# A planned four-stage kernel: the last rows' end by tile, the last FFN block let past the one ahead, and new due times

## The chip, the cores and the metric

The kernel runs on one core of one Trainium2 chip. The metric is the device time of one execution in microseconds (us), the median of several. In the profile PE is TensorE (matmuls), PEld its weight loads, DVE is VectorE, ACT is ScalarE, POOL is GpSimd and SPq is SyncE's queue, from which all transfers are issued.

## The reference, cut to what is computed

The input x is 4 sequences of 1024 rows by 256 features, float32. Four sub-layers follow, each with a residual and a layer norm behind it: a linear attention (stage a), a gated FFN with dequantised weights (stage b), a differential softmax attention with 8 heads (stage c), and a small transformer of two layers (stage d), whose local attention and FFN are what the change touches. Of that last one:

```python
for l in range(2):
    qkv = shift_token(x) @ wqkv                    # 256 -> 3 * 512
    q, k = rotary_xpos(l2norm(q) * qs, l2norm(k) * ksc)
    o = local_attention(q, k, v)                   # 8 heads, windows of 128 rows, each sees itself and the one before
    x = x + o @ wo                                 # 512 -> 256
    h = layernorm(shift_token(x)) * lg + lb
    a, g = split(h @ w1 + b1)                      # 256 -> 2 * 682
    x = x + (a * gelu(g)) @ w2 + b2                # 682 -> 256
x = layernorm(x_before_the_two_layers + x)         # the end of the kernel
```

## The kernel before, in words

The activations x stay in SBUF, as 32 tiles of 128 rows by 256. Float32 products are made of three fp32r products of high and low parts, so an operand is first split: one copy that rounds (the high part) and one subtraction (the low part).

Stage d has, for each of its two layers, 32 windows (one for each tile) and 8 FFN blocks of 4 tiles (512 rows). Blocks are counted through both layers as b = 8 * l + bk, so block 15 is the last one and holds tiles 28 to 31, and block 14 is ahead of it. A window runs d_qk, d_v (projections), d_rope, d_turn, d_sim, d_max, d_exp, d_flip, d_w (attention), d_wo (output), a transfer d_hs that shifts the rows by one, and n_st / n_nm (statistics and normalisation for the FFN). A block runs f_x (two sets of 4 transposes, split into high and low), and then for j = 0 to 5 of the hidden columns f_g, f_a (6 matmuls each; for j = 5 one group holds both), f_ge (GELU on ACT), f_mul (DVE), a split of the hidden part, and f_down (12 matmuls that accumulate in two PSUM banks). f_add adds the two banks to x on DVE, four tiles together. In layer 1 f_r3 (POOL) adds the rows that were kept from ahead of stage d, and n_st / n_nm / store end the block: 4 tiles at a time, with one 512 KB transfer to the output.

The hidden part is split by POOL (f_hp: CAST and subtraction, L2355 and L2357), but in block 15 by ACT (f_hp, L1772) and DVE (f_hl, L2160). The same holds for the rows in f_x.

No engine chooses its order at run time. A planner (class Order) simulates stage d with a cost for each operation (TOOK) and writes each engine's order down. An operation has a due time, PERIOD * window + DUE[...] for windows and PERIOD * (4 * b + 3) + LATE + pace * k for the k-th product of a block. Of the operations that could start within EPS us of the first, the planner takes the one with the lowest due time; so a due time only decides between operations that are ready together. A weight piece is fetched by `fetch` into one of two buffers (SP w_in), is thought to land LANDS us after it, and is then copied on ACT and subtracted on POOL (w_out, L1593 and L2227). In layer 0 the w1 and w2 pieces have the due times FIRST + j * STEP. The engines' queues are in order: an ACT copy that waits for a late transfer holds back all that the planner put behind it.

The products of a block form a chain on PE, and the first of a block comes after the last f_down of the block ahead:

```python
put(len(chain), "pe", kind, *i, after=list(after) + chain[-1:] + ([("pe", "f_down", *before, 5)] if not chain and b else []),
```

SyncE's queue holds all eight stores behind everything else.

## Time and profile before

| | us |
|---|---|
| time, median of 3 runs | 2915.0 |
| lowest and highest | 2911.52, 2915.43 |
| the profiled execution's own time | 2915.99 |
| its span | 2914.1 |

The span is what the trace covers; the profiled execution's own time is 1.9 us longer, and 1.0 us over the median. Stage d begins near 1555 us of the span and takes the rest. PE is busy 97% of the span at a mean granted clock of 0.987, and the second-busiest engine, DVE, 74%.

### The profile page before, as it was taken

What the parts mean: (1) busy time and instruction counts of PE and PEld (TensorE: products, weight loads), DVE (VectorE), ACT (ScalarE), POOL (GpSimd) and SP (SyncE); (2) the same over time, 40 slices, a digit from 0 to 9 for tenths busy, and PEclk for the clock granted to TensorE, in tenths of its full rate; (3) what the DMA queues carried; (4) which work ended last, traced back from release to release, by engine and by line L of the source; (5) the groups of instructions that cost most, each with busy time, mean ns of one, the idle gap of its engine ahead of it and who ended that gap; (6) DMA issues with size and microseconds to landing.
All of it is one profiled execution on the core that took longest, in us unless ns stands there. A gap on an engine that the chain in (4) does not pass through costs nothing.

```text
span 2914.1 us, 52525 instructions
## 1 busy us (share of the span) xinstructions
PE 2819.9 (97%) x20384; PEld 1898.0 (65%) x20384; DVE 2169.0 (74%) x5057; ACT 1651.0 (57%) x3486; POOL 1049.7 (36%) x1208
## 2 busy tenths in 40 slices
PE   8998999999999999999998899999999999999997
PEld 7777877433333333333335778888888878888886
DVE  7885545788788778877874667777777778888884
ACT  3222332665565656556664666666666766666662
POOL 5343442014113211321322334444545554444451
PEclk9999999999999999999999999999999999999998
DMA  2000010320321222042202000000000100000001
GB/s 79 23 9 23 8 22 3 40 28 10 41 23 17 29 28 28 6 59 23 35 11 80 23 5 5 4 5 5 11 27 19 33 27 4 12 11 12 12 11 60
DMA packets 49100, 66.64 MB, mean 23 GB/s; under 512 B 12542, under 2 KB 37076, under 8 KB 48852
## 3 DMA queue, kind: packets, MB, share of 16 engines
q1 hardware_dynamic: 48852, 63.29, 12.2%
q8 instruction: 161, 2.64, 0.4%
q14 instruction: 87, 0.71, 0.1%
HBM read 24.99 MB, written 8.39 MB: 11 GB/s over the span
## 4 chain that ended last, share of the span: by engine, by line
PE 86%; DVE 6%; ACT 3%; DMA 2%; POOL 1%; issue 1%; SPq 1%; POOLq 0%; DVEq 0%; ACTq 0%
PE ps L1394 17%; PE pw L219 17%; PE ps L219 12%; PE pw L1381 11%; PE ps L1180 5%; PE pw L1180 5%; PE ps L1554 4%; PE pw L1467 3%; PE pw L1505 2%; PE pw L1487 1%; PE pw L1330 1%; PE ps L1467 1%; PE ps L1505 1%; PE ps L1487 1%; DMA c_qst<-c_mr 1%
## 5 line engine op out<-in xcount | busy, mean ns | idle before, releaser
L1682 ACT ACTIVATE c_p<-pw 128x512 f32<-128x512 f32 x1024 | 562.3, 595 | 340.5 <-PE ps L1364 183.9
L1394 PE MATMUL ps<-c_p,c_vals 128*64 128x512 f32 x2048 | 548.1, 619 | 3.5 <-ACT c_p L1682 2.2
L1968 DVE TENSOR_REDUCE c_mx<-ps 128x1 f32<-128x512 f32 x694 | 462.7, 683 | 114.1 <-PE ps L1364 106.8
L1381 PEld LDWEIGHTS pw<-c_qst,c_kst 50*128 50x128 f32 x1024 | 154.6, 185 | 368.4 <-ACT c_p L1682 271.9
L1381 PE MATMUL pw<-c_qst,c_kst 50*128 50x512 f32 x1024 | 385.1, 450 | 9.6 <-DMA c_qst<-c_mr 8.4
L1364 PE MATMUL ps<-c_kst,c_qst 48*128 48x512 f32 x694 | 289.3, 452 | 4.4 <-DMA c_kst<-shared 3.5
L1736 ACT ACTIVATE e_sm<-e_sm,e_mx 128x256 f32<-128x256 f32 x512 | 253.9, 498 | 61.8 <-DVE e_mx L2113 61.7
L1968 DVE TENSOR_REDUCE c_mx<-pw 128x1 f32<-128x512 f32 x330 | 225.5, 683 | 47.8 <-PE pw L1364 43.4
L2336 POOL TENSOR_TENSOR e_ss<-e_ss,half 128x16 f32<-128x16 f32 x64 | 186.4, 2912 | 127.9 <-DVE e_ss L2070 84.7
L1394 PEld LDWEIGHTS ps<-c_p,c_vals 128*64 128x64 f32 x2048 | 104.5, 135 | 182.1 <-issue 162.2
L2233 POOL TENSOR_SCALAR stat<-stat 128x1 f32<-128x1 f32 (+1 forms) x138 | 32.2, 233 | 518.1 <-DVE stat L1840 471.5
L219 PE MATMUL pw<-shared,e_xb 128*128 128x512 f32 x774 | 213.1, 412 | 2.3 <-DVE e_xb L2062 1.6
L219 PE MATMUL pw<-shared,e_w 128*124 128x512 f32 (+1 forms) x774 | 204.5, 405 | 1.5 <-ACT e_ge L1781 1.3
L2296 POOL TENSOR_TENSOR c_o<-c_o,c_t 128x128 f32<-128x128 f32 x32 | 14.6, 455 | 487.9 <-DVE c_t L2014 487.9
L2113 DVE CUSTOM_DVE_ANT_0 e_sm<-pw,e_mask,e_ss 128x256 f32<-128x256 f32 x336 | 145.1, 477 | 27.3 <-PE pw L1467 15.3
L1554 PE MATMUL ps<-e_w,e_hp 124*128 124x256 f32 (+1 forms) x1152 | 158.9, 286 | 6.2 <-POOL e_hp L2357 4.6
L219 PEld LDWEIGHTS pw<-shared,e_w 128*124 128x124 f32 (+1 forms) x774 | 140.1, 188 | 36.0 <-ACT e_of L1753 1.5
L219 PEld LDWEIGHTS pw<-shared,e_xb 128*128 128x128 f32 x774 | 138.6, 191 | 30.4 <-DVE e_xb L2062 1.8
L1554 PEld LDWEIGHTS ps<-e_w,e_hp 124*128 124x128 f32 (+1 forms) x1152 | 142.3, 189 | 11.5 <-POOL e_hp L2357 5.3
L1364 PE MATMUL pw<-c_kst,c_qst 48*128 48x512 f32 x330 | 148.7, 450 | 0.0
L1467 PE MATMUL pw<-e_k,e_qt 64*128 64x128 f32 x1344 | 127.9, 280 | 2.6 <-ACT e_pt L1744 1.8
L1364 PEld LDWEIGHTS ps<-c_kst,c_qst 48*128 48x128 f32 x694 | 117.0, 185 | 17.4 <-issue 7.9
(316 smaller groups left out, 6343.5 us busy)
## 6 DMA issues: line engine op xcount, KB each, us to landing
c_kst<-shared SPq DMA_DIRECT2D x192, 64.0 KB
c_qst<-shared SPq DMA_DIRECT2D x64, 128.0 KB
x<-in_L_attn_x SPq DMA_DIRECT2D x8, 512.0 KB, 3.8
c_qst<-shared SPq DMA_DIRECT2D x64, 64.0 KB
keep<-x SPq DMA_DIRECT2D x8, 512.0 KB, 4.0
e_raw<-keep SPq DMA_DIRECT2D x8, 512.0 KB, 3.5
out<-x SPq DMA_DIRECT2D x8, 512.0 KB, 4.7
e_hs<-x SPq DMA_DIRECT2D x64, 63.0 KB
```

Of the source, the lines that this page charges most:

```text
L219: ins = e.matmul(o, l, r, start=first and n == 1, stop=n == 3 * len(parts), skip_group_check=True)
L1180: ins = e.transpose(o, v, ident[0:v.shape[0], 0:v.shape[0]])
L1364: e.matmul(bank_of("c_max", n, sh, qt, h), c_qst[i][p0:p0 + 48, sh // 2, 128 * qt:128 * qt + 128], c_kst[i][p0:p0 + 48, sh // 2, 512 * h:5 ...
L1381: e.matmul(bank_of("c_s", n, sh, kt, h), c_kst[i][p0:p0 + 50, sh // 2, 128 * kt:128 * kt + 128], c_qst[i][p0:p0 + 50, sh // 2, 512 * h:512 ...
L1394: ins = e.matmul(pv[64 * h:64 * h + 64, :], c_v[:, kt, 33 * hd:33 * hd + 64], p[:, 512 * h:512 * h + 512], start=kt == 0, stop=kt == 7, sk ...
L1467: ins = e.matmul(p[r][:, c0:c0 + 128], qt[rs, hb, :], kk[rs, hb, :], start=True, stop=True, skip_group_check=True)
L1554: ins = e.matmul(o, hp[kk, l_, 128 * i:128 * i + 128], d_w2[kk, r, j, :], start=j == 0 and i % 2 == 0 and n == 0, stop=j == 5 and n == 2, ...
L1682: e.activation(c_p[slot["c_p", (n, sh, kt)]][:, 512 * h:512 * h + 512], bank_of("c_s", n, sh, kt, h), ACT.Exp, scale=0.5).then_inc(SC, 1)
L1736: e.activation(sm[:, q, :], sm[:, q, :], ACT.Exp, bias=mx[:, 0, q:q + 1], scale=-1.0, accum_out=mx[:, 1, q:q + 1]).then_inc(SC, 1)
L1968: e.tensor_reduce(c_mx[m % 2][:, qt, h:h + 1], bank_of("c_max", n, sh, qt, h), AX.X, ALU.max).then_inc(VE, 1)
L2113: e.tensor_tensor_reduce(d_sm[s][:, q, :], p[:, 256 * h:256 * h + 256], d_mask[:, 1 if win % 8 else 0, :], st[:, 2, head:head + 1], 3.0e38 ...
L2336: e.tensor_tensor(st[:, 1, :], st[:, 0, :], half[:, :], ALU.pow).then_inc(GP, 1)
```

## The change

It has four parts. (1) The last FFN block by tile: the last f_down of block 15 signals once after its first PSUM bank and again after its second; then f_add, n_st, n_nm and store go tile by tile (stage name "g", tiles 28 to 31), with four transfers of 128 KB in place of one of 512 KB. (2) Block 15's first product no longer has to come after block 14's last f_down, so the planner may put block 15's first products ahead of block 14's last ones; and the hidden parts j = 4 and 5 of block 14 are split by ACT and DVE in place of POOL (`hurried`). (3) LANDS goes from 3.2 to 2.91, FIRST from 10 to 14.83, STEP from 18 to 21.95. (4) LATE and some 25 entries of DUE get new values, so all engines' orders in stage d are planned anew.

```diff
--- before.py
+++ after.py
@@ -16,7 +16,7 @@
 TURN = (0, 2, 1, 3)
-PERIOD, LATE, SPREAD, EPS, LAG = 21, 63.6, 1.36, 0.13, 0.05
+PERIOD, LATE, SPREAD, EPS, LAG, LANDS, FIRST, STEP = 21, 63.09, 1.36, 0.13, 0.05, 2.91, 14.83, 21.95
 TOOK = {"pe d_x": 0.44, "act d_x": 0.62, "dve d_x": 0.72, "dve d_xs": 0.1, "pe d_qk": 1.5, "act d_qk": 0.62,
@@ -33,21 +33,22 @@
-        "dve n_st c": 0.6, "pool n_st c": 0.8, "dve n_nm c": 0.4, "dve n_st b": 3.8, "pool n_st b": 1.4, "dve n_nm b": 1.7,
+        "dve n_st g": 0.6, "pool n_st g": 0.85, "dve n_nm g": 0.42, "dve n_st c": 0.6, "pool n_st c": 0.8, "dve n_nm c": 0.4, "dve n_st b": 3.8, "pool n_st b": 1.4, "dve n_nm b": 1.7,
 BY_HALF = ("d_sim", "d_max", "d_exp", "d_flip", "d_soft", "d_w")
-DUE = {"pe d_qk": 13.7, "act d_qk": 3.7, "dve d_rope": 12.8, "pe d_turn": 5.6, "act d_turn": -19.7, "dve d_ss": 43.6,
+DUE = {"pe d_qk": 13.8, "act d_qk": -0.3, "dve d_rope": 13.2, "pe d_turn": 3.5, "act d_turn": -15.3, "dve d_ss": 31,
-       "pe d_sim1": 19.9, "dve d_max0": 14.6, "dve d_max1": 21.3, "act d_exp0": 16.5, "act d_exp1": 30.3,
-       "pe d_flip0": 5.5, "pe d_flip1": 32.2, "act d_flip0": 31.6, "act d_flip1": -0.2, "dve d_soft0": 20.7,
-       "dve d_soft1": -6.3, "pe d_w0": 25, "pe d_w1": 11.2, "pe d_rb": 42.8, "act d_rb": -19, "dve d_o": 26,
-       "act d_o": 30.9, "dve d_ol": 37.9, "pe d_wo": 15.7, "dve d_wo": 38.1, "dve n_st": 49.9, "pool n_st": 33.8,
-       "dve n_nm": 43.9, "d_x": -1.4}
-LANDS, FIRST, STEP = 3.2, 10, 18
+       "pe d_sim1": 19.9, "dve d_max0": 13.3, "dve d_max1": 28.9, "act d_exp0": 21, "act d_exp1": 30.1,
+       "pe d_flip0": 3.3, "pe d_flip1": 32.2, "act d_flip0": 33.8, "act d_flip1": -6, "dve d_soft0": 20.2,
+       "dve d_soft1": -12.6, "pe d_w0": 23.9, "pe d_w1": 16, "pe d_rb": 43.6, "act d_rb": -34.4, "dve d_o": 28,
+       "act d_o": 43, "dve d_ol": 37.9, "pe d_wo": 21, "dve d_wo": 36.2, "dve n_st": 50, "pool n_st": 38.1,
+       "dve n_nm": 48.7, "d_x": -0.2}
@@ -354,6 +355,10 @@
 
+        def hurried(l, bk, j):
+            return l == 1 and (bk == 7 or bk == 6 and j >= 4)
@@ -972,7 +977,7 @@
 
-                    put(len(chain), "pe", kind, *i, after=list(after) + chain[-1:] + ([("pe", "f_down", *before, 5)] if not chain and b else []),
+                    put(len(chain), "pe", kind, *i, after=list(after) + chain[-1:] + ([("pe", "f_down", *before, 5)] if not chain and 0 < b < 15 else []),
                         **rings)
@@ -987,11 +992,10 @@
                 rows_split = ("dve", "f_xl", *n, 1) if b == 15 else ("pool", "f_x", *n, 1)
-                part_split = ("dve", "f_hl") if b == 15 else ("pool", "f_hp")
 
                 def down(j):
-                    product("f_down", j, after=[(*part_split, *n, j), ("pool", "w_out", ("w2", l, j, 0))],
-                            takes=[(acc, "f_acc", *n, k) for k in range(2 if j == 0 else 0)], gives=[(hps, "f_hp", *n, j)])
+                    product("f_down", j, after=[("dve", "f_hl", *n, j) if hurried(l, bk, j) else ("pool", "f_hp", *n, j), ("pool", "w_out", ("w2", l, j, 0))],
+                            n_of=2 if b == 15 and j == 5 else 1, takes=[(acc, "f_acc", *n, k) for k in range(2 if j == 0 else 0)], gives=[(hps, "f_hp", *n, j)])
 
@@ -1010,7 +1014,7 @@
                         takes=[(hfs, "f_hf", *n, j), (hps, "f_hp", *n, j)], gives=[(bank, both, *n, j)], place=ones if j == 5 else None)
-                    if b == 15:
+                    if hurried(l, bk, j):
                         put(len(chain), "act", "f_hp", j, after=[("dve", "f_mul", *n, j)])
@@ -1021,8 +1025,9 @@
                 hs_read = [("dma", "d_hs", l, t) for t in range(4 * bk, kept + 1)]
-                put(len(chain), "dve", "f_add", n_of=4, after=[("pe", "f_down", *n, 5)] + hs_read + [("pool", "f_r3", bk)] * l,
-                    gives=[(acc, "f_acc", *n, k) for k in range(2)])
+                added = [("pe", "f_down", *n, 5)] + hs_read + [("pool", "f_r3", bk)] * l
+                if b < 15:
+                    put(len(chain), "dve", "f_add", n_of=4, after=added, gives=[(acc, "f_acc", *n, k) for k in range(2)])
                 if l:
@@ -1033,9 +1038,17 @@
                     op(t, "pool", "f_r3", (bk,), 1, [("sp", "r3_in", bk), ("dve", "n_nm", "d", 1, 4 * bk + 3)] + hs_read)
-                    op(t, "dve", "n_st", ("f", bk), 8, [("dve", "f_add", 1, bk)])
-                    op(t, "pool", "n_st", ("f", bk), 2, [("dve", "n_st", "f", bk)])
-                    op(t, "dve", "n_nm", ("f", bk), 4, [("pool", "n_st", "f", bk)])
+                    if b < 15:
+                        op(t, "dve", "n_st", ("f", bk), 8, [("dve", "f_add", 1, bk)])
+                        op(t, "pool", "n_st", ("f", bk), 2, [("dve", "n_st", "f", bk)])
+                        op(t, "dve", "n_nm", ("f", bk), 4, [("pool", "n_st", "f", bk)])
+                        return
+                    for j in range(4):
+                        tile = ("g", 28 + j)
+                        op(t + j, "dve", "f_add", (*n, j), 1, added + [("dve", "f_add", *n, j - 1)] * (j > 0), took=0.44)
+                        op(t + j, "dve", "n_st", tile, 2, [("dve", "f_add", *n, j)])
+                        op(t + j, "pool", "n_st", tile, 2, [("dve", "n_st", *tile)])
+                        op(t + j, "dve", "n_nm", tile, 1, [("pool", "n_st", *tile)])
 
@@ -1101,7 +1114,7 @@
         for i in range(8):
-            P.land(f"x{i}", 1, "store", i)
+            P.land(f"x{i}", 4 if i == 7 else 1, "store", i)
             P.add("store", i)
@@ -1160,7 +1173,7 @@
         def norm_tiles(stage, i):
-            return [i[0]] if stage in ("a", "c") else [24 + 4 * i[0] + t for t in range(4)] if stage == "c4" else [
+            return [i[0]] if stage in ("a", "c", "g") else [24 + 4 * i[0] + t for t in range(4)] if stage == "c4" else [
                 4 * i[0] + t for t in range(4)]
@@ -1543,7 +1556,7 @@
                 w.wait_ge(*pool("w_out", ("w2", l, j, 0)))
-                w.wait_ge(*(dve("f_hl", l, bk, j) if (l, bk) == (1, 7) else pool("f_hp", l, bk, j)))
+                w.wait_ge(*(dve("f_hl", l, bk, j) if hurried(l, bk, j) else pool("f_hp", l, bk, j)))
                 if j == 0:
@@ -1553,7 +1566,8 @@
                                        start=j == 0 and i % 2 == 0 and n == 0, stop=j == 5 and n == 2, skip_group_check=True)
-                ins.then_inc(PE, 1)
+                    if i == 3 or (l, bk, j, i) == (1, 7, 5, 1):
+                        ins.then_inc(PE, 1)
 
@@ -1827,6 +1841,8 @@
                     w.wait_ge(*dve("f_add", 1, i[0]))
+                elif stage == "g":
+                    w.wait_ge(*dve("f_add", 1, 7, i[0] - 28))
                 elif stage != "d":
@@ -2178,12 +2194,12 @@
 
-            def f_add(l, bk):
-                w.wait_ge(*pe("f_down", l, bk, 5))
+            def f_add(l, bk, *one):
                 if l:
                     w.wait_ge(*pool("f_r3", bk))
-                for j in range(4):
+                for j in one or range(4):
                     tile = 4 * bk + j
+                    w.wait_ge(*of("pe", "f_down", (l, bk, 5), j // 2 + 1 if one else None))
                     w.wait_ge(*dma("d_hs", l, tile if tile % 8 == 7 else tile + 1))
@@ -2227,7 +2243,7 @@
             def n_st(stage, *i):
-                st, n = st_of(stage, *i), 1 if stage in ("a", "c", "d") else 4
+                st, n = st_of(stage, *i), 1 if stage in ("a", "c", "d", "g") else 4
                 w.wait_ge(*dve("ident"))
@@ -2490,8 +2506,13 @@
             def store(i):
-                w.wait_ge(*dve("n_nm", "f", i))
-                e.dma_start(xout[:, 4 * i:4 * i + 4, :], x[:, 4 * i:4 * i + 4, :]).then_inc(sems[f"x{i}"], 16)
+                if i < 7:
+                    w.wait_ge(*dve("n_nm", "f", i))
+                    e.dma_start(xout[:, 4 * i:4 * i + 4, :], x[:, 4 * i:4 * i + 4, :]).then_inc(sems[f"x{i}"], 16)
+                    return
+                for t in range(28, 32):
+                    w.wait_ge(*dve("n_nm", "g", t))
+                    e.dma_start(xout[:, t:t + 1, :], x[:, t:t + 1, :]).then_inc(sems["x7"], 16)
 
```

## Rows read from the trace of the kernel before

**Rows 1.** The page, part 1: busy us by engine, share of the span, instructions.
```profile
PE 2819.9 (97%) x20384; PEld 1898.0 (65%) x20384; DVE 2169.0 (74%) x5057; ACT 1651.0 (57%) x3486; POOL 1049.7 (36%) x1208
```

**Rows 2.** Windows: length, busy us of PE, PEld, DVE, ACT, POOL, clock, DMA.
```profile
1560.00:1720.00 160.00, 136.40 (x1139) 115.34 (x1138) 111.31 (x321) 93.19 (x234) 61.32 (x65) 0.92 0.13 40
1720.00:2240.00 520.00, 518.50 (x4484) 450.83 (x4482) 396.89 (x1059) 350.62 (x807) 235.64 (x252) 1.00 0.04 11
2240.00:2420.00 180.00, 174.47 (x1516) 150.70 (x1516) 136.06 (x346) 121.17 (x275) 90.08 (x93) 1.00 0.09 25
```

**Rows 3.** f_add in layer 0 and 1: count, ns min/median/max, first and last start.
```profile
L2188 DVE TENSOR_TENSOR x<-x,ps x16: 415/416/421, 1928.9 to 2169.3; 128x256 f32<-128x256 f32 x16
...
L2188 DVE TENSOR_TENSOR x<-x,ps x20: 412/414/422, 2415.9 to 2737.3; 128x256 f32<-128x256 f32 x20
```

**Rows 4.** Timeline, layer 0's start: start us, us, instruction, idle before and releaser.
```profile
1610.21 0.42 ACT L1593 ACTIVATE e_w<-e_raw 124x256 fp32r<-124x256 f32 x1 [1.12 <-DMA e_raw<-in_L_ffn_w]
...
1611.67 1.11 PE L1180 MATMUL ps<-ident,e_sm 128*128 128x128 f32 x4 [4.15 <-ACT e_sm L1736]
...
1630.90 2.10 PE L1180 MATMUL pw<-ident,e_sm 128*128 128x128 f32 x8 [4.04 <-ACT e_sm L1736]
```

**Rows 5.** Timeline, the last window's normalisation to block 15's first product.
```profile
2860.73 1.56 PE L219 MATMUL ps<-shared,e_w 128*126 128x512 f32 x6
...
2860.91 0.21 DVE L1840 BATCH_NORM_AGGREGATE stat<-stat 128x2 f32<-128x12 f32 x1
...
2862.11 0.61 DVE L1850 TENSOR_SCALAR e_hn<-x,stat 128x128 f32<-128x128 f32 x1 [0.34 <-POOL stat L2235]
...
2862.65 1.42 DVE L1850 TENSOR_SCALAR e_hn<-e_hs,stat 128x128 f32<-128x128 f32 x1
...
2862.73 1.26 POOL L2357 TENSOR_TENSOR e_hp<-e_hf,e_hp 124x512 fp32r<-124x512 f32 x1
...
2864.04 1.63 PE L1554 MATMUL ps<-e_w,e_hp 124*128 124x256 f32 x12 [1.74 <-POOL e_hp L2357]
...
2868.55 1.65 PE L1554 MATMUL ps<-e_w,e_hp 63*128 63x256 f32 x6 [2.88 <-POOL e_hp L2357]
...
2871.41 1.97 PE L1180 MATMUL pw<-ident,e_hn 128*128 128x128 f32 x8
...
2875.82 2.92 PE L219 MATMUL ps<-shared,e_w 128*124 128x512 f32 x6 [2.44 <-DVE shared L2155]
```

**Rows 6.** The same normalisation: 18 earlier ones, and one at 2339.
```profile
L1850 DVE TENSOR_SCALAR e_hn<-e_hs,stat x18: 333/342/660, 2515.9 to 2848.1; 128x128 f32<-128x128 f32 x18
...
2339.69 1.44 DVE L1850 TENSOR_SCALAR e_hn<-e_hs,stat 128x128 f32<-128x128 f32 x1
```

**Rows 7.** Windows of the end: behind POOL stand granted clock, DMA share, GB/s.
```profile
2862.00:2864.00 2.00, 0.30 (x2) 0.00 (x0) 1.89 (x2) 0.68 (x1) 1.91 (x3) 1.00 1.04 335
2870.00:2880.00 10.00, 7.56 (x25) 6.00 (x25) 5.92 (x16) 1.95 (x3) 1.28 (x2) 0.50 0.01 2
2882.00:2900.00 18.00, 18.00 (x104) 15.54 (x103) 8.31 (x16) 6.04 (x10) 0.00 (x0) 1.00 0.09 29
```

**Rows 8.** Timeline of the final product, additions, statistics and normalisation.
```profile
2902.84 1.67 PE L1554 MATMUL ps<-e_w,e_hp 63*128 63x256 f32 x12 [1.58 <-DVE e_hp L2160]
...
2904.55 1.42 DVE L2188 TENSOR_TENSOR x<-x,ps 128x256 f32<-128x256 f32 x4 [1.76 <-PE ps L1554]
...
2906.00 1.41 DVE L1837 BATCH_NORM_STATS2 stat<-x 128x6 f32<-128x256 f32 x4
...
2909.30 1.38 DVE L1854 TENSOR_SCALAR x<-x,stat 128x256 f32<-128x256 f32 x4 [1.49 <-POOL stat L2235]
```

**Rows 9.** Transfers: KB each, median us from issue to landing (last store, a load).
```profile
out<-x SPq DMA_DIRECT2D x1, 512.0 KB, 2.9
...
b_raw<-in_L_attn_Wq SPq DMA_DIRECT2D x2, 128.0 KB, 2.0
```

## The prediction, made before the changed kernel was run

> **What bounds the kernel now.** I read the page first. TensorE (PE) is busy for 97% of the span [rows 1], so an edit is worth something only where PE waits, where it runs at the lower clock, or behind its last product. Then I read the windows, stage by stage. Here the reader is to see three kinds of stretch. In the middle of each layer PE has no free time: 518.50 of 520 us [rows 2]. At the start of layer 0 it has 136.40 of 160 us, at a mean clock of 0.92: 23.6 us idle and some more lost to the clock. At the change from layer 0 to layer 1 it has 174.47 of 180 us, 5.5 us idle [rows 2]. f_add's starts mark the period of a block. Four blocks of layer 0 lie between 1928.9 and 2169.3; the four additions of one start over 1.0 us, so three periods are 239.4, one 79.8 us. Five blocks of layer 1, from 2415.9 to 2737.3, give 320.4 / 4 = 80.1 us [rows 3]. PERIOD is 21 for a window, 84 for a block, so the due times don't set this pace; PE's own work does.
>
> Next I asked the timeline what PE waits for. At layer 0's start its two longest waits, 4.15 and 4.04 us, are for e_sm, the exponentials on ScalarE (ACT). The row of ACT shortly before the first shows a weight copy (L1593) that stood waiting for its transfer, with the exponentials queued behind it [rows 4].
>
> Last comes the end, which is a chain. The last window's normalisation n_nm ends at 2862.65 + 1.42 = 2864.07 us. Block 15's transposes need no more than that, but start at 2871.41, because they are placed behind block 14's last f_down. PE works on two f_down in between, with idle times of 1.74 and 2.88 us for POOL's split of the hidden part [rows 5]. Then the clock falls: it is 0.50 in 2870 to 2880 and 1.00 in 2882 to 2900 [rows 7]. Behind the last f_down there are 2914.1 - (2902.84 + 1.67) = 9.6 us of additions, statistics, normalisation and store [rows 8].
>
> **The change part by part. First, block 15 passing block 14.** (a) f_x no longer waits for block 14. Transposes to first product took 2875.82 - 2871.41 = 4.4 us [rows 5]. Started at n_nm's end, 2864.1, they put the first product at 2868.5: 7.3 us earlier. (b) n_nm itself took 0.61 and 1.42 us while POOL split the hidden part; the second ends as POOL's subtraction ends (2862.73 + 1.26 = 2863.99) [rows 5]. Eighteen earlier ones have a median of 342 ns, and one at 2339, where POOL was also splitting and no store was under way, took 1.44 [rows 6]. With j = 4 split by ACT and DVE, n_nm should end near 2862.11 + 2 * 0.34 = 2862.8, 1.3 us earlier. Bounds: 0 to 1.3; I take 1.3, as both slow rows have POOL beside them. Together 8.6 us. (c) Block 14's last f_down must still be done, now between or behind block 15's products. The twelve matmuls of such an f_down took 1.6 us at the full clock [rows 5]; the j = 4 one fits in the 2.4 us that PE waited between transposes and product, the j = 5 one costs 1.4 (1.6 less the overlap with its neighbour): -1.4 of the gain. (d) The clock. The first six matmuls of block 15 took 2.92 us, and six such at the full clock 1.56 [rows 5]. The low clock lasted until about 2881, so 5.2 us behind 2875.82 held 2.6 us of work. If PE has less idle time ahead of block 15 the whole 2.6 may come back, if not, nothing. Both gaps shrink but one of some 2 us stays, and that is between the ends: I take 1.3. Sum: 8.6 - 1.4 + 1.3 = 8.5 us. Upper end: 8.6 + 0.9 (the transposes took 1.97 us at the low clock, half at the full one) - 1.4 + 2.6 = 10.7. Lower end: (a) alone, 7.3, less 1.4, less 1 for what DVE now does in the same gap (two memsets, f_mul and f_hl of j = 5 beside f_x and f_xl of block 15): 5.
>
> The split's work moves from POOL to ACT and DVE, one copy and one subtraction for each of two parts. I cost it at nothing, since block 15 already does the same beside full PE work (18.00 of 18 us busy, with DVE at 8.31 and ACT at 6.04 [rows 7]). If that cover is gone it is two times 1.3 us. f_down(15, 0) now waits for f_add of block 14 to free both banks; 1.42 us of DVE [rows 8], hidden by f_g and f_a, which come first.
>
> **Second, the end by tile.** Before: additions from 2904.55, n_nm ends 2910.68 [rows 8], then issue, then a 512 KB store of 2.9 us [rows 9]. After: the first bank is ready half an f_down earlier, at 2903.8. A tile costs DVE some 0.36 + 0.40 + 0.21 + 0.35 us and two gaps, 1.4 in all (additions and n_nm by a quarter of their rows [rows 8], the aggregation by [rows 5]); four make 5.6: 2909.4. The last tile must also wait for POOL, 2862.11 - (2860.91 + 0.21) = 0.99 us from statistics to n_nm [rows 5], which makes it 2910.0. So n_nm ends 0.6 to 1.3 us earlier. The last store is 128 KB. A load of that size took 2.0 us [rows 9], 0.9 less; the others go out ahead of it, each in SP's queue behind its own tile's wait, and nothing else is behind them. Gain 1.4 to 2.6; I take 2.0. The Trainium skill, "DMA: Bandwidth & Descriptors", section on the anatomy of one DMA, puts a fixed 2.0 us on each transfer and lets the rest grow with its bytes, measured on GpSimd's path: by it the last store would be an estimated 2.3 us, the gain 0.3 less. That speaks against small transfers; here only the last of the four counts, and no run shows a 128 KB store yet.
>
> **Third, the weight transfers.** Later due times make ACT's copies lose more ties, but ties are within 0.13 us; and LANDS 2.91 lets the planner place a copy 0.29 us earlier than before, where it waited already [rows 4]. At best both waits go: 4.15 + 4.04 = 8.2 us. At worst one more of their kind comes, and the present ones last longer: 4.2 + 2 * 0.3 = 4.8 lost. **Fourth, the due times.** In the middle PE has nothing idle, so only the order of its groups can tell. The two layers differ by 0.3 us for a block [rows 3]; over 13 steady blocks that is 4 us either way. The starts could gain or lose a few us. For both parts I take a gain of 2 us, since waits of 8.2 us lie open there and the middle can't get better than full.
>
> **Sum.** 8.5 + 2.0 + 2.0 = 12.5 us. The profiled execution's own time of 2915.99 becomes 2903.5, and as it stands 1.0 us over the median of 2915.0, I predict 2902.5 us.
>
> **The rivals.** (A) As summed: 2902.5, its own range 2896 to 2909, chance 0.60. (B) The new due times remove both weight waits, 8.2 in place of 2: 2896. For it speaks that the same copy shows in both; against it, that LANDS goes the wrong way. Chance 0.15. (C) The passing brings little: the order is fixed by a plan that thinks the shifted rows land 2.6 us behind d_wo, so if f_x stands first in PE's queue and its rows come late, PE waits with f_down(14, 4) behind it, and the clock stays low. Then 5 + 1.4, and the due times give back 3: 3.4 in all, 2911.6. Chance 0.18. (D) Slower: the new orders put more of ACT's weight copies ahead of exponentials whose transfers are late. Each costs PE 4.1 us [rows 4]. Layer 0 has 12 copies of w1 and w2, layer 1 has 20 of all kinds, and two are seen to hurt now. The ends give back 10.5 us, so four new ones are needed to be slower by over 0.2%: 2915.0 - 10.5 + 4 * 4.1 = 2921. Against it: it must happen four times. Chance 0.07.
>
> A rule that matters to (b): the Trainium skill, "SBUF — State Buffer", section "SBUF: two separate sides", says that a transfer can't slow an engine's access, while VectorE and GpSimd lock each other out of a shared port. The first stores ran in the same microseconds, at 335 GB/s [rows 7]; were they the cause of the 1.42, the 1.3 us would not come and the sum be 11.2. The row at 2339 [rows 6] sides with the page.
>
> **How the numbers follow.** The most likely case is A. Low: 2902.5 less 8.2 - 2 (weights) less 2.2 (clock and transposes) less a little: 2893. High: C, 2912. Some 2 in 10 lie outside. About 0.2%, 5.8 us, is what a measurement of this kernel can tell from no change. A and B nearly whole, less A's upper tail, give faster 0.74; C with that tail gives the same 0.19; D gives slower 0.07.
>
> **What would show it.** In the changed profile: f_x of block 15 (L1180, e_hn) starts within 1 us of n_nm's end and ahead of an f_down; the last n_nm of a window has two pieces of 0.34 us; no POOL e_hp in the last two parts of block 14; block 15's first product within 5 us of n_nm's end; the granted clock above 0.5 behind it; f_down's end to span's end 7.6 us in place of 9.6; the blocks' period 79.8 and 80.1. Idle time of PE in stage d's first 160 us should be between 15 and 28 us. The prediction is wrong if a weight copy's wait shows up more often in those stretches, if the period of a block moves by over 0.3 us, or if PE waits with block 15's transposes at the head of its queue.

## The result, and the profile after

The changed kernel took 2889.68 us (median of 4 runs, 2888.54 to 2893.61) against 2913.39 us beside it: a ratio of 0.9921, 95% interval 0.9904 to 0.9938. That is 23.7 us faster. I had predicted a gain of 12.5 us, from a baseline of 2915.0, to 2902.5 us with a range down to 2893. The direction was right, the size was not. Of the 12.8 us between 2902.5 and 2889.7, 1.6 us are the baseline, which measured 2913.4 here; 11.2 us are the gain.

The page of the changed kernel (span and busy time):

```profile
span 2886.8 us, 52549 instructions
...
PE 2810.2 (97%) x20384; PEld 1890.6 (65%) x20384; DVE 2167.2 (75%) x5059; ACT 1649.1 (57%) x3488; POOL 1054.0 (37%) x1210
```

PE still fills 97% of the span, as in [rows 1]: its busy time and the span shrank together.

To find where the time went, I cut both traces at the same events: stage d's first product (L219 in the kernel before, e_xb, at 1558.78; L220 in the changed one, at 1553.57), f_add of blocks 0, 6, 8 and 13, the last n_nm, the end. The cut at stage d's first product matters. The stages ahead of it are untouched, yet in the profile of the kernel before they took 5.2 us longer than in that of the changed one, and over all 20 profiles of this study they took 1553 to 1559 us. A single profile's span carries that scatter, so the parts are counted from that product on:

| us | before | changed | difference |
|---|---|---|---|
| first product of stage d to block 0's f_add | 210.5 | 200.4 | -10.1 |
| to block 6's f_add (layer 0's middle) | 480.2 | 480.2 | 0.0 |
| to block 8's (change of layer) | 166.4 | 165.9 | -0.5 |
| to block 13's (layer 1's middle) | 400.9 | 398.8 | -2.1 |
| to the second piece of the last n_nm | 45.8 | 46.9 | +1.1 |
| to the span's end | 51.5 | 41.0 | -10.5 |
| sum | 1355.3 | 1333.2 | -22.1 |

So there are two gains of about equal size, at stage d's start and at its end. First the start: f_add (L2204 here) of the changed kernel for block 0, for four blocks of layer 0 and for five of layer 1:

```profile
L2204 DVE TENSOR_TENSOR x<-x,ps x4: 412/414/420, 1754.0 to 1755.0; 128x256 f32<-128x256 f32 x4
...
L2204 DVE TENSOR_TENSOR x<-x,ps x16: 411/414/421, 1833.8 to 2074.1; 128x256 f32<-128x256 f32 x16
...
L2204 DVE TENSOR_TENSOR x<-x,ps x20: 411/414/423, 2400.1 to 2720.2; 128x256 f32<-128x256 f32 x20
```

Block 0 is at 1754.0 - 1553.6 = 200.4 us. The periods are (2074.1 - 1833.8 - 1.0) / 3 = 79.8 us in layer 0, as before, and (2720.2 - 2400.1 - 1.0) / 4 = 79.8 in layer 1, where [rows 3] gave 80.1. Three windows in the start show the difference best. The kernel before, 60 to 80, 120 to 140 and 140 to 160 us behind stage d's first product:

```profile
1618.78:1638.78 20.00, 14.60 (x127) 12.30 (x125) 13.46 (x38) 12.66 (x34) 8.60 (x10) 0.83 0.13 33
1678.78:1698.78 20.00, 16.82 (x108) 13.42 (x108) 11.89 (x31) 12.29 (x26) 9.48 (x10) 0.91 0.00 1
1698.78:1718.78 20.00, 18.05 (x207) 15.95 (x203) 14.04 (x44) 13.89 (x33) 5.89 (x7) 1.00 0.02 5
```

The same three of the changed kernel:

```profile
1613.57:1633.57 20.00, 16.51 (x169) 13.54 (x168) 16.91 (x56) 15.64 (x45) 8.59 (x9) 1.00 0.13 33
1673.57:1693.57 20.00, 18.74 (x164) 15.81 (x163) 15.11 (x42) 13.92 (x32) 11.11 (x11) 1.00 0.02 4
1693.57:1713.57 20.00, 20.00 (x191) 17.10 (x191) 13.38 (x39) 15.82 (x34) 6.15 (x7) 1.00 0.02 6
```

Window by window, counted from the same product: the addition of d_wo (DVE) moved by 1.4 us at most for windows 0 to 2, for window 3 it comes 5.7 us earlier (100.7 and 95.0 us), and from window 7 on 10.1 to 10.5 us (window 9: 220.8 and 210.3). In the three stretches shown PE is busy for 5.8 us more, and the granted clock is 1.00 where it was 0.83 and 0.91.

Over the whole way from stage d's first product to block 0's f_add, the kernel before and the changed one:

```profile
1558.78:1769.28 210.50, 186.89 (x1577) 159.27 (x1578) 148.25 (x424) 127.97 (x314) 82.13 (x86) 0.94 0.11 34
...
1553.57:1753.97 200.40, 183.97 (x1577) 156.31 (x1578) 149.13 (x424) 127.95 (x314) 86.59 (x86) 0.96 0.11 36
```

Both hold the same 1577 matmuls. PE is idle for 210.50 - 186.89 = 23.6 us in the first and 200.40 - 183.97 = 16.4 us in the second, 7.2 us less. Its busy time for the same matmuls falls by the other 2.9 us, beside a mean clock of 0.96 in place of 0.94. So the start's gain is some seven tenths idle time; the rest goes with the clock.

Now the end, to be held against [rows 5]. The changed kernel, from the last n_nm to block 14's last f_down:

```profile
2845.53 0.34 DVE L1866 TENSOR_SCALAR e_hn<-x,stat 128x128 f32<-128x128 f32 x1 [0.35 <-POOL stat L2251]
...
2845.79 0.34 DVE L1866 TENSOR_SCALAR e_hn<-e_hs,stat 128x128 f32<-128x128 f32 x1
...
2846.18 0.66 PE L1193 MATMUL ps<-ident,e_hn 128*128 128x128 f32 x4 [0.89 <-DVE e_hn L1866]
...
2847.03 1.61 PE L1567 MATMUL ps<-e_w,e_hp 124*128 124x256 f32 x12
...
2847.72 1.35 ACT L1779 ACTIVATE shared<-e_hf 128x512 fp32r<-128x512 f32 x2 [1.17 <-DVE e_hf L2165]
...
2848.39 1.75 DVE L2171 TENSOR_TENSOR shared<-e_hf,shared 128x512 fp32r<-128x512 f32 x2
...
2850.19 1.65 PE L220 MATMUL pw<-shared,e_w 128*124 128x512 f32 x6 [1.55 <-DVE shared L2171]
...
2854.54 1.67 PE L1567 MATMUL ps<-e_w,e_hp 63*128 63x256 f32 x12
```

The transposes of block 15 (2846.18) start 0.65 us behind the start of n_nm, ahead of two f_down of block 14. The first product comes at 2850.19, 4.66 us after the start of n_nm at 2845.53; before, it was 2875.82 - 2862.11 = 13.71 us. Block 14's last f_down (63 rows, 2854.54) runs between block 15's products. Two windows, one beside the transposes and one over block 15:

```profile
2846.00:2848.00 2.00, 1.82 (x16) 1.82 (x17) 1.85 (x4) 0.83 (x2) 1.71 (x1) 1.00 1.03 342
2850.00:2876.00 26.00, 24.69 (x138) 20.67 (x138) 16.01 (x35) 8.43 (x13) 1.63 (x2) 1.00 0.17 56
```

The granted clock is 1.00 in both, where it was 0.50 in 2870 to 2880 [rows 7]. Last the tile-wise end, to be held against [rows 8]:

```profile
2876.47 2.58 PE L1567 MATMUL ps<-e_w,e_hp 63*128 63x256 f32 x12 [1.59 <-DVE e_hp L2176]
...
2877.80 0.42 DVE L2204 TENSOR_TENSOR x<-x,ps 128x256 f32<-128x256 f32 x1 [1.39 <-PE ps L1567]
...
2878.72 0.18 DVE L1856 BATCH_NORM_AGGREGATE stat<-stat 128x2 f32<-128x6 f32 x1
...
2879.30 0.57 POOL L2251 TENSOR_TENSOR stat<-stat,half 128x1 f32<-128x1 f32 x1
...
2880.23 0.41 DVE L2204 TENSOR_TENSOR x<-x,ps 128x256 f32<-128x256 f32 x1
...
2881.03 0.41 DVE L1870 TENSOR_SCALAR x<-x,stat 128x256 f32<-128x256 f32 x1 [0.39 <-POOL stat L2251]
...
2881.92 0.39 DVE L2204 TENSOR_TENSOR x<-x,ps 128x256 f32<-128x256 f32 x1
...
2884.13 0.41 DVE L1870 TENSOR_SCALAR x<-x,stat 128x256 f32<-128x256 f32 x1 [0.72 <-POOL stat L2251]
```

The first addition starts 1.33 us after the last f_down's start, before that f_down has ended. Each tile's statistics, POOL step and normalisation follow. The transfers of that window:

```profile
out<-x SPq DMA_DIRECT2D x4, 128.0 KB, 1.7
```

### The profile page after: what moved, and what is told of

Same layout as the page of the kernel before. It is cut to its first block, busy times and chain, and to the rows that moved or that the text cites. A ratio compares the mean times of both kernels' runs of the same rounds, so it can differ in the third digit from the quotient of the medians.

```text
span 2886.8 us, 52549 instructions
## 1 busy us (share of the span) xinstructions
PE 2810.2 (97%) x20384; PEld 1890.6 (65%) x20384; DVE 2167.2 (75%) x5059; ACT 1649.1 (57%) x3488; POOL 1054.0 (37%) x1210
## 4 chain that ended last, share of the span: by engine, by line
PE 88%; DVE 5%; ACT 2%; DMA 2%; POOL 1%; issue 1%; SPq 0%; POOLq 0%; ACTq 0%; DVEq 0%
PE ps L1407 17%; PE pw L220 17%; PE ps L220 13%; PE pw L1394 11%; PE ps L1193 6%; PE pw L1193 5%; PE ps L1567 4%; PE pw L1518 3%; PE pw L1480 2%; PE pw L1500 2%; PE ps L1480 1%; PE ps L1518 1%; PE pw L1343 1%; DMA c_qst<-c_mr 1%; PE ps L1343 1%; DVE c_mx L1984 1%
## 5 line engine op out<-in xcount | busy, mean ns | idle before, releaser
L220 PE MATMUL pw<-shared,e_xb 128*128 128x512 f32 x750 | 205.5, 412 | 2.3 <-DVE e_xb L2078 1.6
L220 PE MATMUL pw<-shared,e_w 128*124 128x512 f32 (+1 forms) x678 | 179.7, 404 | 1.7 <-DVE shared L2171 1.5
L2129 DVE CUSTOM_DVE_ANT_0 e_sm<-pw,e_mask,e_ss 128x256 f32<-128x256 f32 x358 | 153.3, 475 | 15.7 <-PE pw L1480 11.3
L220 PEld LDWEIGHTS pw<-shared,e_xb 128*128 128x128 f32 x750 | 134.7, 191 | 29.3 <-DVE e_xb L2078 1.8
L220 PEld LDWEIGHTS pw<-shared,e_w 128*124 128x124 f32 (+1 forms) x678 | 120.9, 187 | 30.4 <-DVE shared L2171 1.7
L2086 DVE TENSOR_REDUCE e_ss<-e_tq 128x16 f32<-128x1024 f32 x64 | 77.9, 1217 | 67.2 <-ACT e_tq L1732 67.2
```

Source lines behind the costliest of these rows:

```text
L220: ins = e.matmul(o, l, r, start=first and n == 1, stop=n == 3 * len(parts), skip_group_check=True)
L2129: e.tensor_tensor_reduce(d_sm[s][:, q, :], p[:, 256 * h:256 * h + 256], d_mask[:, 1 if win % 8 else 0, :], st[:, 2, head:head + 1], 3.0e38 ...
```

## The experiments

Each is an edit of the changed kernel unless it says otherwise. Times are medians; in brackets stands the kernel before, measured beside the run on the same chip. The parts are cut as above. The period is the mean of the first four in layer 0 and of the last five in layer 1 that are whole. All runs are in one table; the texts below take them in turn.

| run | us (kernel before) | to block 0 | period, layer 0 | period, layer 1 | end |
|---|---|---|---|---|---|
| before | | 210.5 | 79.8 | 80.2 | 51.5 |
| changed | 2889.7 (2913.4) | 200.4 | 79.8 | 79.8 | 41.0 |
| e4: all numbers old | 2903.9 (2914.4) | 210.3 | 79.8 | 80.1 | 40.7 |
| e3: before, all numbers new | 2902.7 (2914.4) | 200.8 | 79.8 | 79.8 | 51.4 |
| e2: DUE and LATE old | 2902.1 (2914.4) | 208.9 | 79.8 | 80.1 | 40.6 |
| e1: LANDS, FIRST, STEP old | 2924.6 (2914.4) | 225.1 | 82.4 | 79.8 | 40.6 |
| f1: LANDS 3.2 | 2920.4 (2912.9) | 225.5 | 82.4 | 79.7 | 40.8 |
| f2: FIRST, STEP old | 2893.3 (2912.9) | 205.3 | 79.8 | 79.7 | 40.6 |
| h1: LANDS 2.6 | 2895.4 (2912.8) | 201.3 | 79.8 | 79.9 | 40.6 |
| g4: LANDS 3.9 | 2946.6 (2913.9) | 227.0 | 82.4 | 81.9 | 42.3 |
| h3: PE's due times old | 2892.3 (2912.8) | 200.4 | 79.8 | 79.7 | 40.5 |
| h4: only PE's due times new | 2902.9 (2912.8) | 208.3 | 79.8 | 80.2 | 40.6 |
| k1: ACT's due times old | 2899.0 (2913.4) | 208.7 | 79.8 | 79.8 | 40.6 |
| k2: DVE's and POOL's old | 2899.2 (2913.4) | 209.8 | 79.2 | 80.1 | 40.6 |
| g1: before, small transfers | 2909.9 (2913.9) | 208.3 | 79.8 | 80.1 | 51.4 |
| g2: small transfers | 2891.0 (2913.9) | 200.8 | 79.8 | 79.8 | 40.6 |
| e5: no passing | 2899.4 (2912.9) | 198.2 | 79.8 | 79.8 | 48.4 |
| e6: POOL splits block 14 | 2891.1 (2912.9) | 200.5 | 79.8 | 79.7 | 41.3 |
| g3: four tiles together | 2891.1 (2913.9) | 198.2 | 79.8 | 79.8 | 41.9 |
| g5: norms last | 2891.2 (2912.8) | 200.9 | 79.8 | 79.7 | 39.7 |

Runs whose start is planned alike differ by up to 2.7 us in "to block 0" (198.2 to 200.9). Two of them, e5 and g3, make that spread: in their first 40 us the granted clock was 0.92 and 1.00, although PE was busy for 18.2 and 15.9 us of each 20, as in the changed kernel. In all other runs of the table it was 0.84 to 0.86 and 0.90 to 0.91, and there the runs planned alike lie between 200.4 and 200.9. So the entries of e5 and g3 are some 2.5 us too good, and the other entries can be compared to about a microsecond.

In e1, f1 and g4 "to block 0" is not a delay alone: PE did 1678 or 1679 matmuls ahead of block 0's f_add in place of 1577, so windows went ahead of the block.

**Which half carries the start?** e4 has the new end and all old numbers, e3 the old end and all new numbers, e2 and e1 one group of numbers each.

```diff
# e4; e3 is the kernel before with the + values; e1 takes back LANDS, FIRST, STEP alone, e2 LATE and DUE alone
-PERIOD, LATE, SPREAD, EPS, LAG, LANDS, FIRST, STEP = 21, 63.09, 1.36, 0.13, 0.05, 2.91, 14.83, 21.95
+PERIOD, LATE, SPREAD, EPS, LAG, LANDS, FIRST, STEP = 21, 63.6, 1.36, 0.13, 0.05, 3.2, 10, 18
-DUE = {new values}
+DUE = {old values}
```

> The changed kernel with all old numbers (DUE, LATE, LANDS, FIRST, STEP): the end alone, as my prediction costed it at 10.5 us. Expected 2902 to 2904, block 0's additions at 1769, last n_nm to span's end 41 to 43 us in place of 52. The rival (the passing is only planned with the new due times): transposes of block 15 still behind block 14's last f_down, 2910 to 2912.

> The kernel before with all new numbers (DUE, LATE, LANDS, FIRST, STEP), its end as it was. If start and end add up, the start's 15 to 17 us come and the end's 10.7 do not: block 0's additions at 1754, last n_nm to span's end 52 us, time 2896 to 2899. If the end's gain needs the new numbers or the other way round, it lies outside this.

> The changed kernel with LANDS, FIRST, STEP back at 3.2, 10, 18; due times and end stay new. Theory W (the gain at layer 0's start, 15.3 us up to block 0's additions, comes from the weight pieces' planned transfers): block 0's additions fall back to 1765 to 1770, the time to 2900 to 2905. Theory D (it comes from the windows' due times): additions stay at 1754 to 1757, time 2889 to 2893. In both the end, from the last n_nm to the span's end, stays 41 us.

> The changed kernel with DUE and LATE as before; LANDS, FIRST, STEP and the end stay new. Theory W: block 0's additions stay near 1754 to 1758, time 2889 to 2895. Theory D: additions go back to 1765 to 1770, time 2900 to 2906. A third one (only the two together were fitted, neither half works alone): this run and the one with old weight numbers both lose over 8 us.

The end alone gives 10.5 us (interval 6.7 to 15.2), and 10.5 was predicted; its profile has the end at 40.7 us, so passing is planned with the old due times too. The numbers alone give 11.7, less than the 15 to 18 us that I had expected of e3: that expectation took block 0's 1769.3 - 1754.0 = 15.3 us with the 5.2 us of stages a to c in it. They add up: 22.2 of 23.7. Of the theories on the start, both simple ones fell. With old due times the three weight numbers (LANDS, FIRST, STEP) change 2903.9 to 2902.1. With new due times they change 2924.6 to 2889.7. The third theory holds: the sets work only together, and the new due times with the old weight numbers are slower than the kernel before (ratio 1.0031, interval 1.0018 to 1.0044).

**Which weight number?** One line each:

```diff
-... LAG, LANDS, FIRST, STEP = ..., 0.05, 2.91, 14.83, 21.95
+... LAG, LANDS, FIRST, STEP = ..., 0.05, 3.2, 14.83, 21.95     # f1; 2.6 in h1, 3.9 in g4
+... LAG, LANDS, FIRST, STEP = ..., 0.05, 2.91, 10, 18          # f2
```

> The changed kernel with LANDS alone back at 3.2. The runs so far: with LANDS, FIRST and STEP all old and the new due times, block 0's additions come 225 us behind stage d's first product in place of 200, and a block of layer 0 takes 82.4 us in place of 79.8. Theory L (the planned landing time carries it, because a copy on ACT must not be planned ahead of its data): this run is bad, 2905 to 2925 us. Theory S (the due times of the pieces do): this run stays at 2888 to 2895, first 200 to 203 us, block 79.8.

> The changed kernel with FIRST and STEP alone back at 10 and 18. Theory S: bad, 2905 to 2925 us, as with all three old. Theory L: 2888 to 2895. A third (any change of one number reshuffles a greedy plan, good or bad by luck): both this run and the one with LANDS alone are off by several us, without order.

> The changed kernel with LANDS 3.9, near what the transfers took where a copy waited (4.16 and 3.70 us). Theory F (a truer cost plans better): at least as good as the changed kernel, 2885 to 2891. Theory O (2.91 is where the due times were fitted, and any other value gives another order): 2895 to 2925, with block 0's additions beyond 205 us or layer 0's period over 80 us.

> The changed kernel with LANDS 2.6. So far 2.91 gives block 0's additions at 200 us, 3.2 at 225 and 3.9 at 227, the last two with a period of 82.4 us in layer 0. Theory M (a monotone rule: the earlier the plan thinks pieces land, the better): 198 to 201 us, period 79.8, 2888 to 2892. Theory O (the due times were fitted at 2.91 and any other order is a draw): over 205 us or a period over 80, 2895 to 2925.

LANDS carries it: 0.29 us in a planner's belief cost 30.7 us, as Theory L had it for f1 and f2. FIRST and STEP are worth 3.6 us. h1 fits neither theory: 2895.4 us is outside Theory M's 2888 to 2892, while block 0 (201.3) and the period (79.8) are as M had them. So an earlier belief isn't better, and not every other order is as bad as 3.2. g4, at 2946.6 us, is the slowest of all, beyond even Theory O's 2925; a larger cost did not plan better. It was a truer cost only in part: 3.9 is near the 4.16 and 3.70 us of two w2 pieces that ACT waited for in the kernel before, but the w1 piece that it waited for landed 3.07 us after its issue (1605.38 to 1608.45). One number stands for both kinds, so whether a true cost for each plans better wasn't tested.

Below are f1's additions of block 0 and of four blocks in layer 0, and how long ACT sat idle ahead of its weight copies (L1607), and how often:

```profile
L2204 DVE TENSOR_TENSOR x<-x,ps x4: 368/414/415, 1782.2 to 1783.1; 128x256 f32<-128x256 f32 x4
...
L2204 DVE TENSOR_TENSOR x<-x,ps x16: 367/414/416, 1864.6 to 2112.7; 128x256 f32<-128x256 f32 x16
...
  DMA e_raw<-in_L_ffn_w: 1.5, 2
```

The period is (2112.7 - 1864.6 - 1.0) / 3 = 82.4 us: the plan falls into another pattern for the rest of layer 0, long after the weights are in. What the pattern is, the traces show in part. ACT loads a table (ACT_TABLE_LOAD) each time that it changes between GELU and the exponentials. The loads ahead of exponentials in three periods of layer 0, in the changed kernel and in f1:

```profile
L1750 ACT ACT_TABLE_LOAD x9 | 11.5, 1283 | 0.2
...
L1750 ACT ACT_TABLE_LOAD x12 | 15.4, 1283 | 0.2
```

The loads ahead of GELU (L1795) are as many. So a block has 6 loads in the changed kernel and 8 in f1, and two more of 1.28 us are 2.6 us, the difference between 79.8 and 82.4. In all of stage d the kernel before, the changed one and all other runs but five have 91 loads; f1 and e1 have 105, g4 115, h1 and k2 93. The planner counts 0.66 us for f_ge and nothing for a load, so it can't see what such an order costs. No run changes the number of loads alone; that they make the longer period is an inference from the match.

ACT's copies waited for their transfers for only 1.5 us, less than in the changed kernel (2.5 us, one wait) and in the kernel before (5.8 us, three). On ACT the planned orders of f1 and of the changed kernel are the same up to one w2 piece of layer 0; right behind it a d_qk copy and a pair of exponentials change places, and from there on they differ.

**Do the transfers themselves matter?** g1 (of the kernel before) and g2 (of the changed one) keep every order and transfer only a part of layer 0's w1 and w2 pieces, and leave out the other columns; only the times are read.

```diff
 for r, s in src:
+    if key in small:      # the w1 and w2 pieces of layer 0
+        o, s = (v[r][:, :, 0:32], s[:, :, 0:32]) if key[0] == "w1" else (v[r][:, 0:64], s[:, 0:64])
+        e.dma_start(o, s).then_inc(landed, 16)
+        continue
     e.dma_start(...)
```

> The kernel before, every order as it was, in which the w1 and w2 pieces of layer 0 transfer only a small part of their columns (32 of 248, 64 of 256; the rest of the raw buffer keeps what it held, so the FFN of layer 0 works with wrong weights). The planner still thinks 3.2 us. Theory T (ACT's copies that wait for transfers cost PE the two stalls of 4.15 and 4.04 us, as the prediction had it): block 0's additions 5 to 8 us nearer to stage d's first product than 210.5 us, time 2905 to 2908. Theory O (the order alone makes the start): 208 to 210 us, time 2911 to 2914.

> The changed kernel with the same cut of layer 0's w1 and w2 transfers, order unchanged. It has one wait of 2.5 us of a copy for its transfer. Theory T: 1 to 3 us faster, block 0's additions at 198 to 199 us. Theory O: no change, 200 us and 2889 to 2891.

In g1 ACT's idle time ahead of weight copies falls from the 5.8 us of the kernel before to:

```profile
  DMA e_raw<-in_L_ffn_w: 2.3, 2
```

3.5 us less waiting brought block 0 forward by 2.2 us, and the time by some 4 us (ratio 0.9988, interval 0.9979 to 0.9998, so 0.6 to 6 us). PE's longest wait for exponentials at the start is now 2.7 us in place of 4.15 and 4.04, but other waits grew: its idle time to block 0 fell only from 23.6 to 20.7 us. In g2 nothing moved that can be told. The waits that I had read in [rows 4] are real, but they are worth a fifth of the start's gain. e2, which has the new weight numbers and the old due times, comes to about the same place by another way: 208.9 us to block 0, 20.9 us idle.

**Whose due times?** h3, h4, k1 and k2 mix DUE by the engine in its key.

```diff
-DUE = {new values}
+DUE = {old values for keys of "pe" (h3) / of all but "pe" (h4) / of "act" (k1) / of "dve" and "pool" (k2), new ones for the rest}
```

> The changed kernel in which only TensorE's due times are as before; those of the other engines, LANDS, FIRST, STEP and LATE are new. If TensorE's own order (when windows give way to block 0) makes the start, block 0's additions go back to 208 to 211 us; if the order on ACT and DVE does, they stay near 200. If the set works only as a whole, they lie beyond 211, or layer 0's period is over 80.

> The other half: only TensorE's due times are new, those of the other engines as before. If TensorE's order makes the start, 200 to 202 us; if the others' does, 208 to 211. If the set works only as a whole, beyond 211 or a period over 80.

> The changed kernel in which only ScalarE's due times are as before. TensorE's alone made no difference to the start (200.4 us to block 0's additions), so those of the other engines carry it. If ScalarE's do, this run has 208 us or more and 2898 to 2905; if VectorE's and GpSimd's do, it has 200 to 202 us and 2889 to 2892.

> The changed kernel in which only VectorE's and GpSimd's due times are as before. The mirror of the run with ScalarE's: 208 us or more and 2898 to 2905 if VectorE's and GpSimd's due times carry the start, 200 to 202 us and 2889 to 2892 if ScalarE's do. If both runs are bad, each half needs the other.

TensorE's own due times do nothing for the start (200.4 with the old ones, 208.3 with them alone new), although TensorE is the busy engine. ScalarE's and VectorE's with GpSimd's do, and only together: 208.7 and 209.8 with either half old. LATE stayed new in all four; d_x, which belongs to no one engine, was new in h3, k1 and k2 and old in h4.

**The end, part by part.** e5 takes back the passing, e6 the faster split of block 14, g3 the end by tile.

```diff
# e5
-([("pe", "f_down", *before, 5)] if not chain and 0 < b < 15 else [])
+([("pe", "f_down", *before, 5)] if not chain and b else [])
# e6
-            return l == 1 and (bk == 7 or bk == 6 and j >= 4)
+            return l == 1 and bk == 7
# g3: f_add, n_st, n_nm ("f", 7) and store(7) as before, one signal behind the last f_down
# g5
-                        op(t + j, "dve", "n_nm", tile, 1, [("pool", "n_st", *tile)])
+                        op(t + 4 + j, "dve", "n_nm", tile, 1, [("pool", "n_st", *tile)])
```

> The changed kernel in which block 15's first product must again come behind block 14's last f_down; ACT/DVE split of block 14's last two parts and the end by tile stay. My account: passing itself is worth 7.3 less 1.4 for the f_down that is done later plus 1.3 to 2.6 of clock, so this run is slower by 5 to 8 us: 2895 to 2898. The rival (the faster split alone closes the gap, so that passing is worth little): 2890 to 2892.

In e5, n_nm, block 14's last f_down, block 15's first transposes, its first product, and the window of 2852 to 2860:

```profile
2848.32 0.35 DVE L1866 TENSOR_SCALAR e_hn<-x,stat 128x128 f32<-128x128 f32 x1 [0.35 <-POOL stat L2251]
...
2852.92 2.63 PEld L1567 LDWEIGHTS ps<-e_w,e_hp 63*128 63x128 f32 x12 [1.86 <-DVE e_hp L2176]
...
2855.78 1.11 PE L1193 MATMUL ps<-ident,e_hn 128*128 128x128 f32 x4
...
2860.18 1.77 PEld L220 LDWEIGHTS pw<-shared,e_w 128*124 128x124 f32 x5 [2.84 <-DVE shared L2171]
```

```profile
2852.00:2860.00 8.00, 4.82 (x20) 4.20 (x20) 4.78 (x9) 1.41 (x3) 0.00 (x0) 0.50 0.46 151
```

n_nm is short, but the first product comes 2860.18 - 2848.32 = 11.9 us after it in place of 4.7. The clock is down again, and f_down takes 2.93 us. The end is 48.4 us, 7.4 more than in the changed kernel's profile and 7.8 more than in most other runs with passing. The time, 2899.4 us, is 9.7 us more than the changed kernel's and beyond the 2895 to 2898 that I had expected; the rest is beyond what the profile's parts show. The rival, under which passing is worth little, is out.

> The changed kernel in which POOL splits all of block 14's hidden parts again, while block 15 may pass. My account: n_nm of the last window is 1.3 us longer beside POOL (pieces of 0.6 and 1.4 us in place of 0.34), f_down(14, 5) is late but off the path: 1.3 to 3 us slower, 2891 to 2893. If the long n_nm came from the stores' traffic and not from POOL, it stays at 0.34 here too.

In e6, n_nm beside POOL, and the first product; then the window around n_nm with the transfers' GB/s last:

```profile
2845.95 0.61 DVE L1866 TENSOR_SCALAR e_hn<-x,stat 128x128 f32<-128x128 f32 x1 [0.35 <-POOL stat L2251]
...
2846.48 1.42 DVE L1866 TENSOR_SCALAR e_hn<-e_hs,stat 128x128 f32<-128x128 f32 x1
...
2846.56 1.26 POOL L2373 TENSOR_TENSOR e_hp<-e_hf,e_hp 124x512 fp32r<-124x512 f32 x1
...
2851.67 0.29 PEld L220 LDWEIGHTS pw<-shared,e_w 128*124 128x124 f32 x2 [1.41 <-DVE shared L2171]
```

```profile
2846.00:2848.00 2.00, 0.18 (x2) 0.04 (x1) 1.90 (x2) 0.68 (x1) 1.74 (x2) 1.00 1.03 334
```

The two pieces are back at 0.61 and 1.42 us. The stores run at 334 GB/s here and at 342 in the changed kernel beside transposes, where both pieces took 0.34. So POOL was the cause and the stores were not, as the Trainium skill, "SBUF — State Buffer", section "SBUF: two separate sides", has it. The first product comes 5.72 us behind n_nm's start, 1.06 later than with the split on ACT and DVE; the time is 1.4 us more, which the timing doesn't tell from none.

> The changed kernel with block 15's additions, statistics, normalisation and store for four tiles together again, the last f_down with one signal; all else stays. The prediction had 2.0 us for the end by tile (1.4 to 2.6): 2891 to 2893. From the last f_down's start to the span's end 11.3 us, as before, in place of 9.4 to 10.3. The rival: eight more hand-overs between engines eat it, 2889 to 2890.

> A try at a better end: in the changed kernel the four normalisations of tiles 28 to 31 are due behind all additions and statistics, so that DVE no longer waits 0.39 and 0.72 us for POOL between tiles. From the last f_down's start to the span's end 9.4 to 9.6 us in place of 10.3, 0.5 to 1 us faster: 2888.5 to 2889.5, which three or five rounds may not tell from 2889.7. The rival: the last tile's POOL step stays at the end of the chain, no change.

The last f_down, the first additions and the normalisation of g3:

```profile
2876.71 1.68 PE L1567 MATMUL ps<-e_w,e_hp 63*128 63x256 f32 x12 [1.58 <-DVE e_hp L2176]
...
2878.43 1.42 DVE L2204 TENSOR_TENSOR x<-x,ps 128x256 f32<-128x256 f32 x4 [1.78 <-PE ps L1567]
...
2883.19 1.38 DVE L1870 TENSOR_SCALAR x<-x,stat 128x256 f32<-128x256 f32 x4 [1.49 <-POOL stat L2251]
```

And of g5, where the four normalisations run as one group behind everything:

```profile
2879.38 2.12 PE L1567 MATMUL ps<-e_w,e_hp 63*128 63x256 f32 x12 [1.58 <-DVE e_hp L2176]
...
2880.39 0.42 DVE L2204 TENSOR_TENSOR x<-x,ps 128x256 f32<-128x256 f32 x1 [1.06 <-PE ps L1567]
...
2884.35 1.58 DVE L1870 TENSOR_SCALAR x<-x,stat 128x256 f32<-128x256 f32 x4
```

From the last f_down's start to the span's end, g3 takes 2888.0 - 2876.71 = 11.3 us, as the kernel before did, the changed kernel 2886.8 - 2876.47 = 10.3, and four other runs (e2, e4, e6, f2) with the end by tile 9.9 to 10.0. (In the changed kernel's profile that f_down ran partly at the lower clock, 2.58 us in place of 1.63.) g5 takes 9.0, less than the 9.4 to 9.6 expected, while its time, 2891.2 us, is above the 2888.5 to 2889.5 expected. So by the profiles the end by tile is worth 1.3 us, and its better order 0.9 us more; the timed medians, 2891.1 for g3 and 2891.2 for g5, can't tell either from the changed kernel. No version that I ran is measurably better than it.

## Why the prediction was wrong

**The end: right in its steps, exact by luck.** The sum was 10.5 us; e4 measures 10.5 with an interval from 6.7 to 15.2, the profile 10.7 from the start of n_nm. (a) and (b), 8.6 us predicted from n_nm to the first product: 13.71 - 4.66 = 9.05 measured, and e6 gives 1.06 of it to (b) where I had 1.3. (c) and (d), -1.4 and +1.3: the way from the first product to the last f_down went from 27.02 to 26.28 us, +0.7 in place of -0.1. The clock stayed up for all of it, which was the upper end of (d). The end by tile was oversized: 1.3 us against 2.0. So the terms of the passing were 1.3 us too small together and the end by tile 0.7 too large (1.0 by the changed kernel's own profile, 11.3 - 10.3), and they nearly cancel. (The sum's 2903.8 for the first bank should be 2902.84 + 0.84 = 2903.7, and its 0.40 us for a tile's statistics stood in no row; neither matters.) The store was better than I had it: 1.7 us for 128 KB, against 2.0 by the load, and against the 2.3 estimated from the Trainium skill's "DMA: Bandwidth & Descriptors", section on the anatomy of one DMA. That figure is for GpSimd's path; this store went out from SyncE's queue and was faster. But n_nm wasn't better: a tile's steps on DVE took 0.42 + 0.43 + 0.18 + 0.41 = 1.4 us, as summed, but between tiles DVE waits for POOL, since the plan puts a tile's n_nm ahead of the next tile's statistics. g5 shows that.

**The weight transfers and due times: the step that failed.** The failed term is the 2.0 us for the third and fourth parts together. They measured 11.6 us in the profile, 10.1 at the start and 1.5 elsewhere, and 11.7 us in e3's time. The two parts have to be taken one by one.

For the third, I bounded the start's gain by the two longest waits, 8.2 us. g1 cuts the transfers and wins 2.2 us, as other waits fill in, and from e4 to e2, where only the three weight numbers are new, the median falls by 1.8 us (no more than the noise of such a pair). So the 2 us would have been about right for this part alone, and the two named waits were not its price.

For the fourth, I put no gain of its own at the start, only "a few us" either way. That is the term that was missing. Between e2 and the changed kernel only the due times and LATE differ, and block 0 comes 8.5 us earlier, the time is 12.4 us shorter. The windows had shown what there was to win: 23.6 us idle in the first 160 us and a clock of 0.92 [rows 2]. I listed it and then didn't use it. Of this, 7.2 us of idle time and 2.9 us beside the lower clock came back, through the order of ACT's and DVE's work. The 7.2 alone would have stayed within 8.2; the sum had no term for the clock at the start.

The sign that I had named could not tell the two sizes apart: PE's idle time in stage d's first 160 us was to lie between 15 and 28 us, and it is 160 - 143.7 = 16.3.

The argument on LANDS failed too. I said that it "goes the wrong way", since the planner would place copies before their data. It does, and it didn't matter: with LANDS 3.2 copies waited less and the kernel was 31 us slower. Case B named the right place and too small a price. The steady part was right in kind, 79.8 and 80.1 becoming 79.8 twice; over layer 1 it gave 2.1 us, within my 4. But that the period would hardly move wasn't safe: f1's 82.4 us was one number away.

**What stays open.** Why ACT's and DVE's new due times only work together, and whether LANDS between 2.91 and 3.2 has a single point at which the plan tips, wasn't settled. Which swap of ACT's or DVE's work in windows 3 to 7 won the idle time wasn't isolated, and neither was the price of a table load.

## What to carry to other kernels

Bound what a new order can win by all the time that the busy engine lacks in the stretch, its idle time and what the lower clock takes, and not by the waits that have a name. A list planner's numbers are one set: the due times are good only with the costs at which they were fitted, and changing one cost alone can cost more than the whole tuning gave (LANDS 3.9, nearer to the w2 pieces' own time: 57 us). Look for what the planner doesn't price at all; here ACT's table loads, of which the slow plans had up to 24 more. At the end of a kernel, let the last block start before the one ahead has finished, and count from its real dependency; here that was the larger part of the end's gain, 7.4 of 10.5 us, and the part that could be forecast.

## What the runs showed that I had not expected

Two plans with the same work for PE, which is 98% busy or more in both, differ by 2.6 us for each block in layer 0's middle (79.8 and 82.4); the slower has two more table loads on ACT in each. TensorE's own due times, between the two sets tried, hardly matter on an engine that is 97% busy, while those of the engines that feed it do. Stages a to c, which no run touched, ended between 1553 and 1559 us after the span's start, so one profile's span is uncertain by some 6 us, and parts should be cut at an event behind the untouched stages.
